# Cross-attention and FFN on one core: TensorE's jobs cut into single products, the queues reordered, the first row's merged weights moved into its turn

## The reference

```
x = x + xattn(layernorm(x), ctx, ctx, Wq, bq, Wk, bk, Wv, bv, Wo, bo)
#   softmax(qh @ kh.T) @ vh per head of 16 values, then @ Wo.T + bo
x = x + ffn(layernorm(x), W1, b1, W2, b2)
#   per row g:  (x[g] @ W1[g].T + b1[g]) @ W2[g].T + b2[g]
```

## Time and profile before

| | us |
|---|---|
| median of three runs | 637.8 (634.3 to 641.44) |
| the profiled execution | 641.85 |
| its span, first to last instruction | 640.1 |
| TensorE busy in it | 582.1 |
| VectorE busy | 444.4 |
| ScalarE busy | 374.7 |
| GpSimd busy | 279.7 |
| mean granted clock of TensorE | 0.936 |

### The profile page before, as it was taken

The page is one execution under the profiler, slowest core; times in us unless marked ns, Lnnn a source line. Parts: engine busy times, 40 slices in busy tenths (PEclk is TensorE's granted clock), DMA queues, the critical chain, the costliest instruction groups (busy, mean ns, idle before and its releaser), DMA issues.

```text
span 640.1 us, 13217 instructions
## 1 busy us (share of the span) xinstructions
PE 582.1 (91%) x4179; PEld 334.2 (52%) x4179; DVE 444.4 (69%) x809; ACT 374.7 (59%) x692; POOL 279.7 (44%) x367
## 2 busy tenths in 40 slices
PE   7799988889998899898998899998998999898988
PEld 7544542345554555555555555555554555343567
DVE  6536787778767598686866688586867797667114
ACT  4102675866666476764756675765766666656730
POOL 4002428443933448244762539244752556103701
PEclk9855897999889899998989999999989999988999
DMA  8702052165232554045240654046241534060200
GB/s 281 199 15 50 34 129 61 47 186 162 72 83 49 187 134 134 2 133 182 57 126 13 219 133 112 22 108 207 66 118 31 191 82 134 2 200 2 86 1 33
DMA packets 34080, 65.29 MB, mean 102 GB/s; under 512 B 9778, under 2 KB 11642, under 8 KB 31994
## 3 DMA queue, kind: packets, MB, share of 16 engines
q1 hardware_dynamic: 34042, 64.81, 34.8%
HBM read 34.65 MB, written 4.44 MB: 61 GB/s over the span
## 4 chain that ended last, share of the span: by engine, by line
PE 61%; DVE 10%; issue 8%; ACT 7%; DMA 6%; SPq 5%; POOL 2%; DVEq 0%; ACTq 0%; POOLq 0%
PE pv L495 15%; PE st L481 10%; PE misc L570 9%; PE misc L615 9%; PE nat L464 8%; DVE neg_max L946 5%; ACT probs L792 3%; SPq L338 3%; PE misc L606 3%; DMA inv_sum<-inv_dram 2%; DVE stats L957 2%; DMA inv_dram<-inv_small 1%; DVE y L1027 1%; ACT odd_sum L840 1%; POOL attnT L1208 1%
## 5 line engine op out<-in xcount | busy, mean ns | idle before, releaser
L946 DVE TENSOR_REDUCE neg_max<-nat 128x1 f32<-128x512 f32 x512 | 336.9, 684 | 121.9 <-PE nat L464 120.2
L792 ACT ACTIVATE probs<-st 128x512 f32<-128x512 f32 x505 | 288.0, 599 | 176.3 <-PE st L481 169.5
L464 PE MATMUL nat<-ks,qs 63*128 63x512 f32 x512 | 249.7, 519 | 14.6 <-DVE neg_max L946 12.7
L481 PE MATMUL st<-qs,ks 64*128 64x512 f32 x505 | 236.7, 501 | 24.1 <-ACT probs L792 23.4
L481 PEld LDWEIGHTS st<-qs,ks 64*128 64x128 f32 x505 | 93.4, 192 | 134.5 <-ACT probs L792 116.5
L495 PE MATMUL pv<-probs,vs 128*32 128x512 f32 x1024 | 143.2, 632 | 1.1 <-ACT probs L792 1.1
L464 PEld LDWEIGHTS nat<-ks,qs 63*128 63x128 f32 x512 | 97.4, 196 | 44.1 <-DVE neg_max L946 36.7
L615 PE MATMUL misc<-w_in 64*128 64x256 f32 x448 | 68.6, 399 | 0.0
L615 PEld LDWEIGHTS misc<-w_in 64*128 64x128 f32 x448 | 42.7, 191 | 32.1 <-issue 27.2
L1199 POOL COPY vs<-v_nat 128x256 f32<-128x256 f32 x32 | 12.1, 398 | 101.1 <-PE pv L495 77.2
L570 PE MATMUL misc<-wo_in,attnT 64*128 64x256 f32 x224 | 32.2, 405 | 9.3 <-POOL attnT L1208 9.3
(11 more groups left out here) (161 smaller groups left out, 759.9 us busy)
## 6 DMA issues: line engine op xcount, KB each, us to landing
w_in<-w SPq DMA_DIRECT2D x8, 1024.0 KB
w_in<-w2T SPq DMA_DIRECT2D x8, 1024.0 KB
ks<-hi SPq DMA_DIRECT2D x64, 128.0 KB, 2.4
qs<-hi SPq DMA_DIRECT2D x64, 128.0 KB, 2.4
x_in<-x SPq DMA_DIRECT2D x8, 512.0 KB, 3.4
ctx_in<-ctxT SPq DMA_DIRECT2D x8, 512.0 KB, 3.7
ks<-lo SPq DMA_DIRECT2D x32, 128.0 KB, 2.4
qs<-lo SPq DMA_DIRECT2D x32, 128.0 KB, 2.4
```

The costliest lines, as they stand in the source:

```text
L464: mm(ring(at)[:, :], qs[rows, 2 * g + jj, c * P:(c + 1) * P], ks[rows, 2 * g + jj, :], start=True, stop=True).then_inc(nat_done, 1)
L481: mm(st_of(u, prep)[:, :], ks[rows, 2 * g + jj, kc * P:(kc + 1) * P], qs[rows, 2 * g + jj, :], start=True, stop=True).then_inc(st_done, 1)
L792: act.activation(probs[kc % 2][:, j, :], st_of(u, prep)[:, :], ACT.Exp).then_inc(exp_done, 1)
L946: dve.tensor_reduce(neg_max[:, g % 2, col:col + 1], ring(at_nat(n))[:, :], AX.X, ALU.max, negate=True).then_inc(max_done, 1)
```

## The change

TensorE's jobs are cut finer: a part of K and Q is now one product (2 matmuls) and one of WO, V, Z one step of a contraction, and tables (`K_AT` and so on) name a unit for each, so that 2 to 4 of them stand in a unit. Most jobs begin one or two units earlier. `w21` of row 0 is made in turn 0 as for every other row, and in the lead-in its place behind each `nat` from the third on is taken by `keep_warm`, two half-array products whose result nobody reads. Units of the small operations on ScalarE and VectorE move along. VectorE's combination of a pair reads the copy `odd_sum` instead of the PSUM bank, so that `pv` waits for the copy. SyncE's and GpSimd's turns get another order. The diff, cut to its core:

```diff
-K_UNITS = (5, 6, 8, 9)
-WO_UNITS = (20, 21, 23, 24)
-B2_UNIT = 50
+XT_AT = (0, 1)
+K_AT = (3, 3, 4, 4, 4, 5, 8, 8, 8, 8, 9, 9)
+Q_AT = (11, 12, 12, 12, 13, 13, 15, 15, 16, 16, 17, 17)
+WO_AT = (18, 19, 20, 20, 23, 24, 25, 25)
+V_AT = (29, 29, 29, 29, 31, 32, 32, 33)
+YT_AT = (36, 37)
+Z_AT = (39, 39, 41, 41, 43, 43, 44, 44)
+W21_AT = (48, 51, 52, 53, 55, 55, 56, 57, 58, 58, 59, 60, 60, 60, 61, 61)
+B2_UNIT = 48
+EVEN_AT = (20, 52)
+MASK_AT = (25, 58)
+ODD_AT = (36, 2)
+PAIR_AT = (39, 6)
+INVERT_AT = (51, 7)
+Y_NORM_AT = (30, 33)
+CTX_AT = 57
+X_STATS_AT = (28, 41)
+X_AGGREGATE_AT = 47
+X_NORM_AT = (54, 59)
...
             def turn(b, post, prep, load):
                 if post:
+                    stack_quad(b, 3)
                     gather_sums(b - 1, 1)
                 store_max(b, 1)
-                if post:
-                    stack_quad(b, 3)
-                if load:
-                    wait_apart(sp, norm_ready[0], 4 * (b + 2))
-                    load_x(b + 2)
                 if post:
                     save_inverse(b - 1, 1)
                     spread_inverse(b - 1, 1)
...
                 store_max(b, 2)
+                if load:
+                    wait_apart(sp, norm_ready[0], 4 * (b + 2))
+                    load_x(b + 2)
                 if prep:
                     stack_quad(b + 1, 0)
+                gather_sums(b, 0)
+                if prep:
+                    stack_quad(b + 1, 1)
+                store_max(b, 3, prep)
                 if load:
                     wait_apart(sp, ctx_ready, b + 2)
                     load_ctx(b + 2)
-                if prep:
-                    stack_quad(b + 1, 1)
-                gather_sums(b, 0)
-                store_max(b, 3, prep)
-                save_inverse(b, 0)
-                spread_inverse(b, 0)
                 if post:
                     store_out(b - 1, 0)
                     store_out(b - 1, 1)
+                save_inverse(b, 0)
                 if prep:
+                    store_max(b + 1, 0)
                     stack_quad(b + 1, 2)
                 load_y(b)
-                if prep:
-                    store_max(b + 1, 0)
+                spread_inverse(b, 0)
...
+            def keep_warm(n):
+
+                for t in range(2):
+                    rows = slice(HALF * t, HALF * t + HALF)
+                    mm(misc[t][:, :], w_hi[rows, WK, 0, 0:P], w_hi[rows, WQ].rearrange("p f d -> p (f d)"),
+                       start=True, stop=True)
...
+            def qk_piece(job, which, i):
+
+                phase, f, n = i // 6, i % 6 // 3, i % 3
                 src, w = ((normedT_hi, normedT_lo), WQ) if which == 0 else ((ctx_hi, ctx_lo), WK)
+                left, right = TERMS[n]
+                for t in order(phase):
+                    m, rows = t ^ phase, TILES[t]
+                    last = mm(misc[m][:, :], (w_hi, w_lo)[left][rows, w, f, m * P:(m + 1) * P], src[right][rows, f, :],
+                              start=(i == 0), stop=(i == 11))
...
                 nat(0, n)
-                if n == 0:
-                    pe.wait_ge(ffn_loaded, 64)
-                if n < F * OC:
-                    w21_part(n, n // OC)
+                if n > 1:
+                    keep_warm(n)
...
-                dve.scalar_tensor_tensor(pair_ctx[:, :], pv_bank[:, :], half_hi[:, 0:1], even_ctx[:, :],
+                dve.scalar_tensor_tensor(pair_ctx[:, :], odd_sum[:, :], half_hi[:, 0:1], even_ctx[:, :],
                                          ALU.mult, ALU.add).then_inc(odd_out, 1)
...
                 if post:
                     inverse_root(1, b - 1)
                     add_b2(b - 1)
+                b2_parts(b)
+                if load:
+                    inverse_root(0, b + 2)
                 if prep:
                     v_stack(b + 1, 0)
                     v_stack(b + 1, 1)
-                b2_parts(b)
+                add_bo(b)
+                divide(b, 0)
                 if load:
                     ctx_rest(b + 2)
-                    inverse_root(0, b + 2)
-                divide(b, 0)
                 if prep:
                     v_stack(b + 1, 2)
-                add_bo(b)
```

More of the change, by code:

```diff
@@ L281, in maxT_of, with pieces @@
             return (b, n // 16 - 1) if n <= UNITS else (b + 1, (n - UNITS) // 16 - 1)
+        def pieces(at, u):
+            return [i for i, where in enumerate(at) if where == u]
         CONSTS_QK = 4 * 16
@@ L491, in pv @@
                     else:
-                        wait(pe, odd_out, pair)
+                        wait(pe, odd_copied, pair)
                 wait(pe, exp_done, UNITS * b + 4 * n + 4)
@@ new lines, in jobs @@
+                if post:
+                    for i in pieces(WO_AT, u):
+                        if i == 0:
+                            wait(pe, w21_ready, b)
+                            wait(pe, b2_ready, b)
+                            wait(pe, raw_ready[0], 2 * b + 2 if prep else 0)
+                            wait(pe, attn_ready, 2 * b)
+                        if i == 4:
+                            crossed("wo", 2 * b, 1)
+                        rows_piece("wo", (attnT,), [lambda rows, f: wo_in[rows, f, :]], i, wo_done)
@@ new lines, in jobs @@
+                if prep and u == B2_UNIT:
+                    wait(pe, out_ready, 2 * b if post else 0)
+                    wait(pe, v_ready, 2 * b + 4)
+                    b2sum(b)
+                for i in pieces(W21_AT, u):
+                    if i == 0:
+                        wait(pe, out_ready, 2 * b if post else 0)
+                        wait(pe, ffn_loaded, 64 * (b + 1))
+                    if i == OC:
+                        crossed("w21", 2 * b + 2, 1)
+                    w21_piece(i, prep)
@@ L700, in turn @@
                     if u % 4 == 2:
-                        if prep and u == B2_UNIT:
-                            wait(pe, out_ready, 2 * b if post else 0)
-                            wait(pe, v_ready, 2 * b + 4)
-                            b2sum(b)
                         if u > 4:
@@ L899, in turn @@
-                    if not prep and u == 57:
+                    for pair in range(2):
+                        if u == EVEN_AT[pair]:
+                            even_quad(b, pair)
+                        if u == MASK_AT[pair]:
+                            mask_even(b, pair)
+                    if not prep and u == MASK_AT[1] + 1:
                         wait(act, sums_in, 32 * (2 * b + 1))
+                        wait(act, odd_out, 2 * b + 1)
                         act.activation(odd_sum[:, :], even_sum[:, :], ACT.Copy,
@@ L902, in turn @@
                                        scale=half_hi[:, 0:1]).then_inc(last_even, 1)
-                    if post and u == 62:
+                    if post and u == Y_NORM_AT[0]:
+                        wait(act, xT_done, 2 * (b + 2) if prep else 0)
+                        wait(act, yT_done, 2 * (b - 1))
+                    for half in range(2):
+                        if post and u == Y_NORM_AT[half]:
+                            normalise(1, b - 1, y, 2 * half, 2 * half + 2)
+                    if u == ODD_AT[0]:
+                        odd_quad(b, 0)
@@ new lines, in turn @@
+                    if post and u == YT_AT[-1]:
+                        yT_copy(b - 1, 0, 0)
+                    if load and u == CTX_AT:
+                        ctx_split(b + 2)
+                    if load and u == X_NORM_AT[0]:
+                        wait(act, yT_done, 2 * b if post else 0)
+                        wait(act, xT_done, 2 * (b + 2))
+                    for half in range(2):
+                        if load and u == X_NORM_AT[half]:
+                            normalise(0, b + 2, x_in, 2 * half, 2 * half + 2)
@@ L1062, in turn @@
                             aggregate(1, b - 1)
-                    if prep and u in (32, 33):
-                        v_copy(b + 1, u - 32, u - 32)
-                    if u == 35:
+                    for half in range(2):
+                        if prep and u == V_AT[-1] + half:
+                            v_copy(b + 1, half, half)
+                    if u == PAIR_AT[0]:
                         odd_quad(b, 0)
-                    if post and u == YT_UNITS[-1]:
+                    if post and u == YT_AT[-1]:
```

233 lines of the change are left out of this document (87 added, 146 removed).

## The result

The changed kernel takes 603.2 us (median of four runs, 601.44 to 606.16) where four runs of the kernel before have 636.75: ratio 0.947, 95% interval 0.940 to 0.954, so 33.5 us less. The profiled execution took 601.44, its span is 599.6. It is the fastest of its runs, while the profiled execution of before (641.85) lies above all of its own, so the spans differ by more, 40.5.

What follows compares the result with a forecast made beforehand. TensorE was in front, but no engine full, since they take turns waiting. Lead-in -16.5, turn 0 -1, six turns -28.9, last turn -2.9: -49.3, span 640.1 to 590.8, median 588, range 565 to 612.

Steps and rivals of the forecast that it cites:

- Lead-in: Before turn 0: without w21, VectorE's 0.61 us per maximum sets the pace; 16.5 us less, bounds 10.6 and 17.5.
- rival 3: Lead-in: the clock stays at half despite the fill, costing 0 to 6 us; chance 4 in 10.
- The pace of a group: TensorE's groups from pv to pv: evenly loaded, each takes 3.8 us, 60.8 a turn.
- rival 1: K and b2: the new waits don't come; turn 62.4 to 63, 560 to 568 us; chance 0.15.
- WO without a wait: WO in each turn: the inverse of the denominators comes earlier, so the 1.85 us wait goes; cost 0.
- The wait at K: Turn's start: K's first product waits for ctx_rest, behind load_y, add_bo and divide; 2 us, bounds 0 and 4.
- The wait at b2: Sum of b2, moved to unit 48: TensorE waits for b2_parts on GpSimd; 2 us, bounds 0 and 3.
- 0.7 falls a turn: TensorE's clock in the turns: each fall to half costs about 1.7 us, together 1.2 us a turn.
- The crowd behind WO: VectorE, units 25 to 27: two y halves with statistics stay as they were; +0.8 us a turn.
- Turn 0 and the last turn: First and last turns: turn 0 1 us less, bounds -4 and +3; last turn 2.9 less.
- Rival 2: Turns: the gain is mostly given back by waits, clock falls and slower groups; 606 to 620 us; chance 0.21.
- Rival 4: K: slower than before if its wait exceeds 10 us in each of six turns; chance 0.03.

Runs made afterwards that it cites:

- best version: Changed kernel with ctx_rest ahead of add_bo, b2sum and first w21 piece at unit 51, first half of y's norm at unit 32: 568.2 us, ratio 0.891.
- the mends: Changed kernel with ctx_rest ahead of add_bo and divide on GpSimd, and b2sum and the first w21 piece in unit 51: 576.0 us, ratio 0.903.

## Why the prediction was right, and where it was too large

588 was forecast with 565 to 612 about it; it became 603.2. Of these 15 us, 8.8 are in the span and the rest came from the scaling. The median was set 4.05 below the profiled execution, as in the kernel before, but this time the profiled execution was 1.8 below the median.

*Lead-in.* Right, 18.6 instead of 16.5, and turn 0 begins at 42, not 43.1. The clock came back, so rival 3 fell, and it would have cost nothing here: without the fill `nat` keeps VectorE's pace at half clock too (eight in 4.75 us, 0.6 each). With the fill and still at half clock `nat` and its pair came 0.66 us apart (27.48 to 30.80, five of them), so the estimate of 0.64 was right, and the 0.86 behind the bound of 10.6 too high. The sum had a slip: 27.5 and 16.2 are 43.7, not 43.1.

*The pace of a group.* Right as an average: 3.8 was put, and six ordinary groups have 3.76. The best version, without the three waits, bears it out: a turn of 63.55, where rival 1 (no waits) had 62.4 to 63. Two readings behind it were off. The row group of 3.70 us held six of Q's twelve products, half and not two thirds, and the tables don't give 2 to 6 pieces to each group but up to eight (`w21`, in the group from unit 58 on).

*WO without a wait.* Right, 0.2 us in all.

*The wait at K.* Right in place and chain: 2 us were put, 1.8 found in the mean; in the turn shown load_y is issued 5.1 us behind store_max (5.1 was put), y lands 3.3 later (3.2), and ctx_lo ends 4.4 us into the turn (4.8). *The wait at b2.* Right: 2 put, 1.9 found. What was too low is the clock: I took 0.7 falls a turn, the trace has it at b2 in five of six turns and at K in one more, six in six turns, as many as the kernel before. Stop and fall together are what the mends gave back, 27 us for two waits that sum to 22.5.

*The crowd behind WO* was mis-sized: +0.8 was put, 2.5 found. I had said that it stays as it was, and looked at VectorE only. The norm of y moved to unit 30 while TensorE's units got shorter, and GpSimd's four small operations in front of it (var_eps to shift, 409.80 to 411.86) did not. ScalarE stands, and TensorE after it. Moving it by two units gave 7.8 us, and the same four groups take 16.4 instead of 17.7 us in turn 5 of the best version: 1.3 of the 2.5 were this wait, and the 1.2 left are near the 0.8 that was put.

*The groups of w21* were mis-sized: 3.8 was put, 4.2 found. Fifteen of the sixteen pieces stand in three of the last four groups, three, four and eight. Spreading them as five, five and six changed nothing, and taking two of them away only 0.7 us, so here it is not the unevenness that costs. That it is their number is likely, not shown.

*Turn 0 and the last turn* brought more than was put, 2.0 instead of 1 and 5.1 instead of 2.9; what in them did it was not looked into.

Together: 66.8 + 1.7 (crowd) + 1.7 (w21) - 1.1 (K, b2 and clock, 4.1 in this turn instead of 5.2) = 69.1 a turn, as measured. Rival 2 (turns of 70 to 71, 606 to 620) missed by a little. Rival 4 needed 10 us a turn at K.

*What the prediction didn't ask* is what each part is worth alone. It took the single products as the gain, the new waits as its small change. It is the reverse: the other engines' orders and units brought 28.8 us, the lead-in 14.9, and the single products, with the earlier units that came with them, cost 8.7 and bring 20 once the three waits are gone. Of the 20 a part is not their evenness, but a collision on ScalarE that the old units of xT bring with them, 1.0 of 2.9 us in the turn shown.

## What to carry to other kernels

When work is moved earlier by a unit or two, ask of each first part when its input is finished, on the clock of the engine that makes it: the chains on GpSimd and SyncE don't shrink when TensorE's pace does, and each new stop of 2 us can cost the clock as well. An engine at half load can set the end: look at what stands in its queue behind an operation that waits for a DMA, and let whatever has its input pass it. When work is put back to old units to test an idea, look at what else hangs on these units: here a copy on ScalarE moved along and took part of the credit. When a change of many parts gives less than its model, time its main idea alone, with and without the waits, before it is called weak: here it brought 20 us or cost 8.7, depending on three other lines.

## What the runs showed of the hardware

In the lead-in without the fill TensorE's records cover 12.84 of 13 us with `nat`, at a granted clock of 0.50, 1.2 GHz; with the fill 12.80 of 13, at a mean of 0.89, which is half clock for some 2.9 us and full clock, 2.4 GHz, for the rest. So the profile's busy column doesn't tell the two apart; it overstates the load, since the ends of matmuls are modelled, and in the first case the starts of `nat` follow VectorE, 0.6 us apart. What differs is the work: 23 records against 69, and products on both halves of the array. `w21` with `nat` stayed at 0.50 too. The Trainium skill, "TensorE: Matmul & The Clock Gate", in "What's actually happening", has activity release the throttle; the clock did rise with the fill, and by these rows the busy column is no sign that it will. What in the added products did it wasn't tried.

The other way, a stop of 1.8 to 2.1 us at b2 went with a fall of the clock in five of six turns of the changed kernel, in four with ctx_rest ahead and in three without the fill; with b2 later, and the stop gone, there was none at that place. In the changed kernel's one turn without it the groups of units 46 to 53 took 9.0 us, with it 10.6 (10.57 to 10.65 in the five): some 1.6 us for a fall, near the 1.7 estimated.
